# Four 64-row by 64-column products in place of two wide ones for the third hidden group, and one inverse transform moved ahead of a mix

## The chip, the cores and the metric

The kernel runs on one core of a Trainium2 chip. The metric is the device time in microseconds (us). TensorE (PE in the profile, PEld its weight loads), VectorE (DVE), ScalarE (ACT), GpSimd (POOL) and SyncE (SP) each work through a queue of their own and wait for one another by counting semaphores.

## The reference

A block of two residual parts over an image tensor (4, 48, 128, 128). `_ln_c` normalises over the 48 channels, `_ln_t` over the 48 channels of a token (a pixel).

```python
x = x + conv_part(_ln_c(x))        # conv_part, below
t = _to_tokens(x)                  # (4, 16384, 48)
t = t + ffn(_ln_t(t))
x = _from_tokens(t, x)

# conv_part(x): 3x3 convolution of the first 12 channels, 1x1 convolution 48 -> 254,
# 8x8 patches: rfft2, times fft_w, irfft2; halves a, b of 127 channels each;
# gelu(a) * b, 1x1 convolution 127 -> 48
# ffn(x): with q_mul = rounding to 5 exponent and 2 mantissa bits, q_acc to 5 and 10
h = relu(q_acc(q_acc(q_mul(x) @ q_mul(W1).T) + q_mul(b1)))    # 48 -> 192
y = q_acc(q_acc(q_mul(h) @ q_mul(W2).T) + q_mul(b2))          # 192 -> 48
```

## The kernel before

The images are cut into 32 bands of 16 rows (`STEPS`). A band's 16 rows are two bands of 8 rows laid on top of each other: partitions 0 to 47 hold the 48 channels of the upper, partitions 64 to 111 those of the lower (`HALF` is 64). Every step of the software pipeline works on seven bands at once, each in another stage: `live(t, d)` asks whether the band that is `d` behind exists, `at(t, d)` is its number. Steps 6 to 31 have all stages; before them the pipeline fills, after them it drains, and behind step 34 a separate `drain` works in half bands. The order of each engine's work within a step is written out by hand in that engine's `step` function, and waits on semaphore counts hold the engines together.

What stands around the change, for one step:

- `mix(t, s)`, s = 0 to 3: the 1x1 convolution to 254 channels for a quarter of the band, 16 matmuls of 60 rows (two row halves of the array at a time) into the PSUM pair `mixp` (or `misc0` and `misc1` for s = 1). `weigh(t, s)` on VectorE multiplies both banks by the frequency weights into `gmix[s % 2]`, and counts `gmix_ready` by two. Mix s waits for the weighing of s - 1 (mix 1, which has banks of its own, does not).
- `inverse(t, behind, s)`: the inverse transform of quarter s into `inva` (line 532, 8 matmul records) and `invb` (line 539, 8 records). `inva` waits for `gelu_ready` of quarter s - 1, `invb` for `h_ready` of quarter s - 1, which `gate` on VectorE counts. `gelu` on ScalarE turns `inva` into `gact`, and `gate` multiplies it with `invb` into `hbuf`.
- `turn_rest` transposes the first residual sum into `misc2` and `misc3` (line 663); `rest` on ScalarE copies it (`tpix`) and squares it (`tsq`); `second_norm` on VectorE (lines 1301 to 1313) makes the statistics from both, and GpSimd centres the tokens in between (line 1580, `tcen`), behind its addition into the output buffer (line 1538, `ob`).
- `hidden(t, c, g, dst)`: first layer of the feed-forward part for half c (512 pixels) of a band, output group g of three (line 619). The layer has 192 outputs for each of the two stacked bands, 384 in all. Groups 0 and 1 are outputs 0 to 127 of the upper and of the lower band, 48 rows each, in different row halves of the array. Group 2 is outputs 128 to 191 of both, by a block-diagonal weight of 112 rows and 128 columns. `accumulators` on ScalarE rounds the bank to `hid16`, `relu` on VectorE adds the bias, `activations` on ScalarE rounds to `hid8` in the next step, `second_layer` sums all three groups into `mixp`.
- `stream(t)`: the 3x3 convolution (line 568) into `misc3`; `convs` on ScalarE copies it, `convolve` (line 577) transposes it.

TensorE's order in the second half of a step, before: `turn_rest`, mix 2, hidden (0,0), hidden (0,1), `inva` of quarter 1, hidden (0,2) into `misc2`, `invb` of quarter 1, `stream`, mix 3, hidden (1,0), (1,1), (1,2), `convolve`, inverse of quarter 2; then the next step begins with the transposes of line 784.

ScalarE's order there: `tokens`, `rest`, accumulators (0,0) to (0,2), gelu of quarter 1, `convs`, accumulators (1,0) to (1,2), `zpix` (line 1122), gelu of quarter 2.

VectorE's order there: gate 0, weigh 2, `second_norm`, relu of half 0, gate 1, weigh 3, relu of half 1, gate 2.

Of the kernel before, what the change touches and what calls it, by code (L numbers as in the profile page):

```python
# [10 lines left out]
ALU = mybir.AluOpType  # L11
# [69 lines left out]
def metaformer_kernel(nc, x, w_pc, w_in, fft_w, w_out, w1, b1, w2, b2, fwd_d, inv_d, sel_d, eye_d, out):  # L81
    with ExitStack() as ctx:
# [404 lines left out]
        def _(pe):  # L487
# [111 lines left out]
            def rows(t, behind):  # L599
# [7 lines left out]
                if a < ROWS_EARLY:  # L607
                    pe.wait_ge(tsq_ready, upto(2 * m + 2))
                else:
                    pe.wait_ge(gmix_ready, upto(8 * n + 2))  # L610
                    pe.wait_ge(y16_ready, upto(2 * at(t, 6) + 2))
                dst = bank[3] if a < ROWS_EARLY else mixp[0]
                pe.transpose(dst[0:32, 0:128], rm[:].rearrange("p a j i -> p (a j i)"), eye[:])\
                  .then_inc(rmT_done, 1)

            def hidden(t, c, g, dst):

                r0, r1 = ((0, CH), (HALF, SPAN), (0, SPAN))[g]
                pe.matmul(dst[:], l1h[r0:r1, g, :], q16[r0:r1, 4 * c:4 * c + 4, :], start=True, stop=True,  # L619
                          skip_group_check=True).then_inc(hid_done, 1)  # L620

            def second_layer(t):
# [6 lines left out]
                for c in range(2):  # L629
                    for g in range(2):  # L630
                        r0 = HALF * g
                        pe.matmul(pair[c][r0:r0 + HALF, :], l2[:, g, r0:r0 + HALF], hid8[:, 3 * c + g, :],  # L632
                                  start=True, stop=False, skip_group_check=True)
                for c in range(2):
# [3 lines left out]
                    for r0 in (0, HALF):  # L638
                        mm = pe.matmul(pair[c][r0:r0 + HALF, :], l2[:, 2, r0:r0 + HALF], hid8[:, 3 * c + 2, :],  # L639
                                       start=False, stop=True, skip_group_check=True)  # L640
                    mm.then_inc(y_done, 1)
# [26 lines left out]
            def drain():  # L668
# [20 lines left out]
                def first_layer(k, c, dst):  # L689
                    pe.wait_ge(q16_ready, 2 * k + c + 1)  # L690
                    for g in range(3):
                        hidden(t, c, g, dst[g])

                def second_layer_half(c, dst):
                    for g in range(2):
# [9 lines left out]
                pe.wait_ge(lo_ready, 2 * STEPS)  # L705
                pe.wait_ge(h_ready, 4 * NEW + 2)
                project_half(0, bank[3])

                def between():
                    pe.wait_ge(hid8_ready, 6 * OLDER + 3)  # L710
                    second_layer_half(0, mixp[0])

# [9 lines left out]
                pe.wait_ge(y16_ready, 2 * OLDER + 1)  # L722
                second_layer_half(1, mixp[0])
                pe.wait_ge(tpix_ready, 2 * NEW + 1)
# [36 lines left out]
            def step(t):  # L761
# [14 lines left out]
                if live(t, 0):  # L776
# [5 lines left out]
                    pe.wait_ge(xord_ready, upto(a + 1))  # L782
                    for i in range(PAIRS):
                        mm = pe.transpose(bank[i // 4][:, (i % 4) * 128:(i % 4) * 128 + XSPAN],  # L784
                                          xord[:, i * PX:(i + 1) * PX], eye[0:XSPAN, 0:XSPAN])
# [72 lines left out]
                if a == 2:  # L858
# [25 lines left out]
        def _(act):  # L884
# [5 lines left out]

            def accumulators(t, c, groups):

                k = at(t, 5)
                for g in groups:
                    act.wait_ge(hid_done, upto(6 * k + 3 * c + g + 1))
                    act.wait_ge(hid8_ready, upto(6 * (k - 1) + 3 * c + g + 1))
                    act.activation(hid16[:, 3 * c + g, :], bank[g][:], ACT.Copy).then_inc(hid16_ready, 1)  # L897

            def activations(k, c, groups):

                for g in groups:
                    act.wait_ge(relu_ready, upto(6 * k + 3 * c + g + 1))
                    if c == 0 and g == 0:
                        act.wait_ge(y_done, upto(2 * k))
                    act.sem_inc(act_held, 1)
                    act.activation(hid8[:, 3 * c + g, :], hid16[:, 3 * c + g, :], ACT.Copy, saturate=False)\  # L906
                       .then_inc(hid8_ready, 1)
# [72 lines left out]
            def drain():  # L980

                def convert(k, c, g, tile=None):
                    act.wait_ge(relu_ready, 6 * k + 3 * c + g + 1)
                    act.wait_ge(y_done, 2 * (k - 1) + c + 1)
                    act.activation(hid8[:, 3 * c + g, :], hid16[:, 3 * c + g, :], ACT.Copy, saturate=False)\
# [72 lines left out]
            def step(t):  # L1058
# [29 lines left out]
                if live(t, 6):  # L1088
                    activations(l, 0, range(3))
                    activations(l, 1, range(3))  # L1090
                if live(t, 6):
# [42 lines left out]
        def _(dve):  # L1134
# [134 lines left out]

            def relu(t, c, parts=((0, 2), (2, 1))):  # L1270

                k = at(t, 5)
                for g, size in parts:
                    dve.wait_ge(hid16_ready, upto(6 * k + 3 * c + g + size))
                    buf = hid16[:, 3 * c + g:3 * c + g + size, :]
                    dve.tensor_scalar(buf, buf, bq[:, g // 2:g // 2 + 1], 0.0, ALU.add, ALU.max)\
                       .then_inc(relu_ready, size)

# [36 lines left out]
            def drain():  # L1315
# [57 lines left out]
                def convert(k, c, g):  # L1373
                    dve.wait_ge(relu_ready, 6 * k + 3 * c + g + 1)
                    dve.wait_ge(y_done, 2 * (k - 1) + c + 1)
                    dve.tensor_copy(hid8[:, 3 * c + g, :], hid16[:, 3 * c + g, :], saturate=False).then_inc(late_hid8, 1)
# [47 lines left out]
            def step(t):  # L1424
# [56 lines left out]
                if live(t, 3):  # L1481
                    gate(t, 3, 0)
                if live(t, 3):
                    weigh(t, 2)
                if live(t, 4):
                    second_norm(t)
# [163 lines left out]
```

## Time and profile before

| | |
|---|---|
| timed runs, median of 3 | 700.97 us (700.77 to 700.98) |
| profiled execution, first to last instruction (span) | 699.4 us |
| busy share of the span | PE 95%, PEld 76%, DVE 85%, ACT 77%, POOL 65% |
| granted TensorE clock, mean | 0.980 of full speed |

No separate time of the profiled execution stands in the profile; its span is 1.6 us under the median of the timed runs, and this much is taken as what lies around it. Engine busy shares are averages; a busy PE counts pipelined matmuls, so that the start-to-start distances of blocks of matmuls say more than their durations.

### The profile page before, as it was taken

The numbers are of one execution on the slowest core, as the hardware profiler recorded it, in microseconds if no ns is written. First come the engines' busy times: TensorE is split into PE (matmuls) and PEld (weight loads), VectorE is DVE, ScalarE is ACT, GpSimd is POOL, SyncE is SP. The second block draws the span as 40 slices with busy tenths as digits, with TensorE's granted clock in tenths as the row PEclk, the third lists the DMA queues.
The fourth block names the chain that finished last, engine by engine and source line by source line (L and its number), as shares of the span: only waits on it lengthen the run. The fifth ranks groups of instructions, "written<-read, shape, count | busy, mean of one in ns | idle before, by whom it ended". The sixth has DMA issues, their size and how long they took to land.

```text
span 699.4 us, 19176 instructions
## 1 busy us (share of the span) xinstructions
PE 666.5 (95%) x6620; PEld 529.3 (76%) x6620; DVE 597.9 (85%) x1159; ACT 536.8 (77%) x1087; POOL 456.9 (65%) x347
## 2 busy tenths in 40 slices
PE   4879999999999999999999999999999999999984
PEld 4657877778778877787878877787788777887751
DVE  7637889988988899988988899889888999877877
ACT  4244568888888888888889888888888888877784
POOL 2605677767777777677776877677777876753353
PEclk9989999999999999999999999999999999999995
DMA  4434445444544554445444544545445543342102
GB/s 102 79 78 118 121 113 131 112 126 128 142 120 118 142 140 121 114 120 138 127 123 131 139 131 107 132 121 144 121 116 144 139 129 103 100 119 87 47 23 68
DMA packets 52207, 80.73 MB, mean 115 GB/s; under 512 B 20823, under 2 KB 36079, under 8 KB 52111
## 3 DMA queue, kind: packets, MB, share of 16 engines
q1 hardware_dynamic: 50031, 78.56, 43.2%
q10 hardware_dynamic: 2080, 0.94, 0.6%
q8 instruction: 54, 0.88, 0.6%
q14 instruction: 42, 0.34, 0.2%
HBM read 63.17 MB, written 16.30 MB: 114 GB/s over the span
## 4 chain that ended last, share of the span: by engine, by line
PE 87%; DVE 3%; DMA 3%; issue 2%; ACT 1%; SPq 1%; POOL 1%; DVEq 0%; ACTq 0%; POOLq 0%
PE inva L532 17%; PE invb L539 15%; PE mixp L519 13%; PE misc L548 8%; PE misc L803 8%; PE misc L619 4%; PE misc L519 4%; PE misc L663 3%; PE misc L784 3%; PE misc L568 2%; PE misc L577 2%; PE misc L653 2%; PE mixp L632 2%; PE mixp L639 2%; DMA xin<-in_x_dram 1%
## 5 line engine op out<-in xcount | busy, mean ns | idle before, releaser
L1555 POOL TENSOR_TENSOR st<-st,neg_half 128x16 f32<-128x16 f32 x32 | 93.3, 2915 | 129.2 <-DVE st L1459 129.2
L532 PEld LDWEIGHTS inva<-inv,gmix 128*127 128x127 f32 x1024 | 123.4, 191 | 25.3 <-issue 16.6
L532 PE MATMUL inva<-inv,gmix 128*127 128x128 f32 x1024 | 141.0, 281 | 0.6 <-DVE gmix L1234 0.6
L1234 DVE TENSOR_TENSOR gmix<-mixp,freq_w 128x508 f32<-128x508 f32 x192 | 122.6, 680 | 16.9 <-PE mixp L519 16.9
L539 PE MATMUL invb<-inv,gmix 128*127 128x128 f32 x1024 | 134.7, 274 | 0.1
L539 PEld LDWEIGHTS invb<-inv,gmix 128*127 128x127 f32 x1024 | 126.2, 191 | 2.1 <-DVE hbuf L1245 0.5
L897 ACT ACTIVATE hid<-misc 128x512 f16<-128x512 f32 x180 | 94.1, 599 | 17.7 <-PE misc L619 17.7
L1245 DVE TENSOR_TENSOR hbuf<-gact,invb 127x512 f32<-127x512 f32 x128 | 87.4, 683 | 22.2 <-ACT gact L889 17.7
L1584 POOL TENSOR_TENSOR st<-st,neg_half 128x16 f32<-128x16 f32 x31 | 95.4, 3077 | 16.4 <-DVE st L1313 15.9
L906 ACT ACTIVATE hid<-hid 128x512 fp8e5<-128x512 f16 x174 | 93.2, 619 | 0.0
L889 ACT ACTIVATE gact<-inva 127x512 f32<-127x512 f32 x128 | 77.5, 605 | 19.9 <-PE inva L532 19.3
L519 PE MATMUL mixp<-win,zh 60*128 60x254 f16 x768 | 89.9, 272 | 0.7 <-DVE gmix L1234 0.6
L519 PE MATMUL mixp<-win,zl 60*128 60x254 f16 x768 | 89.0, 267 | 0.0
L1538 POOL TENSOR_TENSOR ob<-tch,y 112x1024 f32<-112x1024 f32 x29 | 62.1, 2140 | 34.1 <-DVE y L1294 34.1
L977 ACT ACTIVATE y<-mixp 112x512 f16<-112x512 f32 x58 | 31.4, 594 | 47.0 <-PE mixp L639 47.0
L803 PE MATMUL misc<-fwd,zpix 128*124 128x128 f32 x512 | 62.1, 275 | 0.0
L548 PE MATMUL misc<-hbuf,wout 127*64 127x512 f32 x248 | 60.1, 605 | 0.0
L803 PEld LDWEIGHTS misc<-fwd,zpix 128*124 128x124 f32 x512 | 58.6, 188 | 0.0
L519 PEld LDWEIGHTS mixp<-win,zh 60*128 60x128 f16 x768 | 37.1, 93 | 26.8 <-issue 14.5
L1435 DVE TENSOR_REDUCE st<-xpix 128x16 f32<-128x768 f32 x32 | 30.5, 952 | 28.3 <-ACT xpix L1068 28.3
L1580 POOL TENSOR_TENSOR tcen<-tpix,st 128x768 f32<-128x768 f32 x31 | 45.7, 1475 | 12.5 <-DVE st L1301 9.6
L1068 ACT ACTIVATE xpix<-misc 128x384 f32<-128x384 f32 x64 | 31.6, 494 | 23.2 <-PE misc L784 22.1
(184 smaller groups left out, 1358.2 us busy)
## 6 DMA issues: line engine op xcount, KB each, us to landing
taps<-cz_scratch SPq DMA_DIRECT2D x63, 292.2 KB
xin<-in_x_dram SPq DMA_DIRECT2D x64, 192.0 KB, 3.3
xres<-in_x_dram SPq DMA_DIRECT2D x64, 192.0 KB, 4.1
out_dram<-ob SPq DMA_DIRECT2D x60, 192.0 KB, 2.6
taps<-cz_scratch SPq DMA_DIRECT2D x63, 146.1 KB
crm<-rm_scratch SPq DMA_DIRECT2D x58, 96.0 KB
cx<-in_x_dram SPq DMA_DIRECT2D x32, 96.0 KB
cz_scratch<-cz SPq DMA_DIRECT2D x63, 48.8 KB
```

The lines of the kernel that those rows point to most:

```text
L519: mm = pe.matmul(pair[q][:, e * HID2:(e + 1) * HID2], zpart[r0:r0 + KC, 2 * s + e, :], win[r0:r0 + KC, wpart, :], start=(e == 0 and zpart ...
L532: mm = pe.matmul(inva[0:HID, q * PX:(q + 1) * PX], gmix[:, s % 2, q, 0:HID], inv[:], start=True, stop=True, skip_group_check=True)
L539: mm = pe.matmul(invb[0:HID, q * PX:(q + 1) * PX], gmix[:, s % 2, q, HID:HID2], inv[:], start=True, stop=True, skip_group_check=True)
L548: mm = pe.matmul(dst[HALF * j:HALF * j + HALF, :], wout[:], hbuf[:, half, j, :, :], start=True, stop=True, skip_group_check=True)
L803: mm = pe.matmul(bank[(3, 0)[i // 4]][0:KSPAN, (i % 4) * PX:(i % 4 + 1) * PX], zpix[:, ring(t, 3), i, 0:KSPAN], fwd[:], start=True, stop=True,
L889: act.activation(gact[:, s % 2], inva[0:HID, :], ACT.Gelu).then_inc(gelu_ready, 1)
L897: act.activation(hid16[:, 3 * c + g, :], bank[g][:], ACT.Copy).then_inc(hid16_ready, 1)
L906: act.activation(hid8[:, 3 * c + g, :], hid16[:, 3 * c + g, :], ACT.Copy, saturate=False)\
L1234: dve.tensor_tensor(gmix[:, s % 2, 2 * q:2 * q + 2, 0:HID2], pair[q][:, 0:2 * HID2].rearrange("p (e c) -> p e c", e=2), freq_w[:], ALU.mul ...
L1245: dve.tensor_tensor(hbuf[:, s // 2, :, 2 * e:2 * e + 2, :], gact[:, s % 2].rearrange("p (j i c) -> p j i c", j=2, i=2), invb[0:HID, :].rea ...
L1555: pool.tensor_tensor(st1[:, 6, :], st1[:, 5, :], neg_half[:], ALU.pow).then_inc(pow1, 1)
L1584: pool.tensor_tensor(st2[:, 6, :], st2[:, 5, :], neg_half[:], ALU.pow).then_inc(pow2, 1)
```

## The change

The third group of the first layer is now computed by `hidden_rest`, once for both halves of the band: four matmuls of 48 rows and 64 columns, each in one quadrant of the array, the lower band into `misc3` and the upper into `misc2`, half c of the band at output partitions 64 c. `hid16` and `hid8` keep six slots in a new order: slots 0 and 1 are half 0, slots 2 and 3 the third group of the lower and of the upper band, slots 4 and 5 half 1. The second layer follows (`rest_product`). `inverse(t, 3, 1)` stands ahead of mix 2 in one piece. `stream` now also waits for `hid16_ready`, 6 k + 3, since `misc3` is read by the third accumulator copy of the step. ScalarE has gelu 1 ahead of the accumulators, four of which now stand in one row ahead of `convs`. VectorE's order becomes gate 0, `second_norm`, gate 1, weigh 2, relu of slots 0 and 1, weigh 3, relu of slots 2 and 3, relu of slots 4 and 5, gate 2.

```diff
@@ stream(t)
+                if live(t, 5):
+                    pe.wait_ge(hid16_ready, 6 * at(t, 5) + 3)
                 pe.wait_ge(col_in, upto(64 * (c + 1)))
...
+            def hidden_rest(t):
+
+                for c in range(2):
+                    for j in (1, 0):
+                        r0 = HALF * j
+                        mm = pe.matmul(bank[2 + j][HALF * c:HALF * c + HALF, :], l1h[r0:r0 + CH, 2, r0:r0 + HALF],
+                                       q16[r0:r0 + CH, 4 * c:4 * c + 4, :], start=True, stop=True,
+                                       skip_group_check=True)
+                        if c == 1:
+                            mm.then_inc(hid_done, 1)
...
+            def rest_product(dst, c, j):
+
+                r0, o = HALF * c, HALF * j
+                return pe.matmul(dst[o:o + HALF, :], l2[:, 2, r0:r0 + HALF], hid8[:, (3, 2)[j], :],
+                                 start=False, stop=True, skip_group_check=True)
...
@@ TensorE, step(t)
                 if live(t, 3):
+                    inverse(t, 3, 1)
+                if live(t, 3):
                     pe.wait_ge(y16_ready, upto(2 * l + 2))
...
-                def last_group():
-                    if live(t, 0) and 3 <= a < ROWS_EARLY:
-                        rows(t, 0)
-                    if live(t, 5):
-                        pe.wait_ge(tsq_ready, upto(2 * m + 1, 2 * STEPS))
-                        hidden(t, 0, 2, bank[2])
-
-                if live(t, 3):
-                    inverse(t, 3, 1, last_group)
-                else:
-                    last_group()
+                if live(t, 5):
+                    pe.wait_ge(tsq_ready, upto(2 * m + 2, 2 * STEPS))
+                    hidden_rest(t)
+                if live(t, 0) and 3 <= a < ROWS_EARLY:
+                    rows(t, 0)
...
                     hidden(t, 1, 1, bank[1])
-                    pe.wait_ge(hid16_ready, upto(6 * k + 3))
-                    hidden(t, 1, 2, bank[2])
@@ ScalarE
-                    act.activation(hid16[:, 3 * c + g, :], bank[g][:], ACT.Copy).then_inc(hid16_ready, 1)
+                    act.activation(hid16[:, g, :], bank[(0, 1, 3, 2, 0, 1)[g]][:], ACT.Copy).then_inc(hid16_ready, 1)
...
+                if live(t, 3):
+                    gelu(t, 3, 1)
                 if live(t, 5):
-                    accumulators(t, 0, (0,))
+                    accumulators(t, (0, 1))
+                if live(t, 5):
+                    accumulators(t, (2, 3))
                 if live(t, 0) and 3 <= a < ROWS_EARLY:
                     rows(t, 0)
-                if live(t, 5):
-                    accumulators(t, 0, (1, 2))
-                if live(t, 3):
-                    gelu(t, 3, 1)
...
-                    accumulators(t, 1, range(3))
+                    accumulators(t, (4, 5))
@@ VectorE
                     gate(t, 3, 0)
-                if live(t, 3):
-                    weigh(t, 2)
                 if live(t, 4):
                     second_norm(t)
+                if live(t, 3):
+                    gate(t, 3, 1)
+                if live(t, 3):
+                    weigh(t, 2)
                 if live(t, 5):
                     relu(t, 0)
-                if live(t, 3):
-                    gate(t, 3, 1)
                 if live(t, 3):
                     weigh(t, 3)
                 if live(t, 5):
                     relu(t, 1)
+                    relu(t, 2)
```

The drain's waits and its older half of the second layer follow the new slots.

## Rows read from the trace of the kernel before

**Rows 1.** The page: the span, and each engine's busy time.
```profile
span 699.4 us, 19176 instructions
PE 666.5 (95%) x6620; PEld 529.3 (76%) x6620; DVE 597.9 (85%) x1159; ACT 536.8 (77%) x1087; POOL 456.9 (65%) x347
```

**Rows 2.** The chain that ended last, middle of one step: start, us, what.
```profile
351.77 1.08 PE inva L532 x8
352.85 0.22 PE misc L619
...
355.51 0.54 PE misc L619 x3
...
356.49 0.89 PE inva L532 x8
```

**Rows 3.** Timeline of the same step, TensorE: start, us, engine, line, what.
```profile
338.32 0.83 PE L784 MATMUL misc<-eye,xord 96*128 96x96 f32 x8
...
350.50 0.28 PE L519 MATMUL mixp<-win,zh 60*128 60x254 f16 x2
...
353.89 0.65 PE L568 MATMUL misc<-taps,wpc 108*32 108x512 f16 x8
354.47 0.28 PE L519 MATMUL mixp<-win,zh 60*128 60x254 f16 x2
...
355.35 0.70 PE L619 MATMUL misc<-q,l1h 48*128 48x512 f16 x3
...
358.10 0.82 PE L784 MATMUL misc<-eye,xord 96*128 96x96 f32 x8
```

**Rows 4.** Timeline of the same step, ScalarE.
```profile
352.19 0.48 ACT L967 ACTIVATE tsq<-misc 128x384 f32<-128x384 f32 x1
352.55 1.55 ACT L897 ACTIVATE hid<-misc 128x512 f16<-128x512 f32 x3
353.98 0.60 ACT L889 ACTIVATE gact<-inva 127x512 f32<-127x512 f32 x1
...
355.76 1.57 ACT L897 ACTIVATE hid<-misc 128x512 f16<-128x512 f32 x3 [0.58 <-PE misc L619]
```

**Rows 5.** Timeline of the same step, VectorE.
```profile
350.70 0.68 DVE L1245 TENSOR_TENSOR hbuf<-gact,invb 127x512 f32<-127x512 f32 x1
...
353.81 0.80 DVE L1307 SCALAR_TENSOR_TENSOR st<-st 128x16 f32<-128x16 f32 x1
354.65 0.17 DVE L1310 SCALAR_TENSOR_TENSOR st<-st 128x16 f32<-128x16 f32 x1
...
355.60 0.68 DVE L1245 TENSOR_TENSOR hbuf<-gact,invb 127x512 f32<-127x512 f32 x1
356.20 1.27 DVE L1234 TENSOR_TENSOR gmix<-mixp,freq_w 128x508 f32<-128x508 f32 x2
```

**Rows 6.** Timeline of the same step, GpSimd.
```profile
350.86 2.14 POOL L1538 TENSOR_TENSOR ob<-tch,y 112x1024 f32<-112x1024 f32 x1 [0.36 <-DVE y L1294]
353.11 1.48 POOL L1580 TENSOR_TENSOR tcen<-tpix,st 128x768 f32<-128x768 f32 x1
```

**Rows 7.** Timeline of step 32, the first without new input.
```profile
629.55 1.47 POOL L1580 TENSOR_TENSOR tcen<-tpix,st 128x768 f32<-128x768 f32 x1 [2.02 <-DVE st L1301]
```

**Rows 8.** Windows while the pipeline fills: stretch, us, busy (count) of PE, PEld, DVE, ACT, POOL, clock.
```profile
29.59:33.00 3.41, 3.41 (x19) 3.41 (x18) 2.65 (x8) 2.00 (x10) 3.22 (x4) 0.50 0.64 177
33.00:39.82 6.82, 2.99 (x27) 2.18 (x26) 0.32 (x1) 0.73 (x1) 1.34 (x1) 1.00 0.98 193
39.83:46.65 6.82, 5.96 (x22) 4.77 (x23) 1.13 (x4) 2.05 (x6) 0.00 (x0) 0.50 0.14 38
```

**Rows 9.** Timeline of TensorE around its second fall in clock.
```profile
37.17 0.65 PE L568 MATMUL misc<-taps,wpc 108*32 108x512 f16 x8 [2.48 <-DMA taps<-cz_scratch]
37.75 0.71 PE L583 MATMUL misc<-eye 128*128 128x128 f32 x4
40.69 1.11 PE L577 MATMUL misc<-eye,convs 128*128 128x128 f32 x4 [2.22 <-ACT convs L1114]
```

More of the change, by code:

```diff
@@ L611, in rows @@
                     pe.wait_ge(y16_ready, upto(2 * at(t, 6) + 2))
+                if live(t, 5) and a < ROWS_EARLY:
+                    pe.wait_ge(hid16_ready, 6 * at(t, 5) + 3)
                 dst = bank[3] if a < ROWS_EARLY else mixp[0]
@@ L629, in second_layer @@
                 for c in range(2):
[L630 to L634, printed above, removed]
                     if c == 1:
@@ L637, in second_layer @@
                         pe.sem_inc(pe_held, 1)
-                    for r0 in (0, HALF):
-                        mm = pe.matmul(pair[c][r0:r0 + HALF, :], l2[:, 2, r0:r0 + HALF], hid8[:, 3 * c + 2, :],
-                                       start=False, stop=True, skip_group_check=True)
+                    for g in range(2):
+                        r0 = HALF * g
+                        pe.matmul(pair[c][r0:r0 + HALF, :], l2[:, g, r0:r0 + HALF], hid8[:, 4 * c + g, :],
+                                  start=True, stop=False, skip_group_check=True)
+                for c in range(2):
+                    for j in range(2):
+                        mm = rest_product(pair[c], c, j)
                     mm.then_inc(y_done, 1)
@@ L692, in first_layer, with older_half @@
                         hidden(t, c, g, dst[g])
+                def older_half(c, dst):
+                    for g in range(2):
+                        r0 = HALF * g
+                        pe.matmul(dst[r0:r0 + HALF, :], l2[:, g, r0:r0 + HALF], hid8[:, 4 * c + g, :],
+                                  start=True, stop=False, skip_group_check=True)
+                    for j in range(2):
+                        mm = rest_product(dst, c, j)
+                    mm.then_inc(y_done, 1)
                 def second_layer_half(c, dst):
@@ L706, in drain @@
                 pe.wait_ge(h_ready, 4 * NEW + 2)
+                pe.wait_ge(hid16_ready, 6 * OLDER + 3)
                 project_half(0, bank[3])
                 def between():
-                    pe.wait_ge(hid8_ready, 6 * OLDER + 3)
-                    second_layer_half(0, mixp[0])
+                    pe.wait_ge(hid8_ready, 6 * OLDER + 4)
+                    older_half(0, mixp[0])
                 inverse(t, 4, 3, between)
@@ L722, in drain @@
                 pe.wait_ge(y16_ready, 2 * OLDER + 1)
-                second_layer_half(1, mixp[0])
+                older_half(1, mixp[0])
                 pe.wait_ge(tpix_ready, 2 * NEW + 1)
@@ L783, in step @@
                     for i in range(PAIRS):
+                        if i == 4 and not peeled:
+                            pe.wait_ge(hid16_ready, upto(6 * l + 6))
                         mm = pe.transpose(bank[i // 4][:, (i % 4) * 128:(i % 4) * 128 + XSPAN],
@@ L889, in gelu, with accumulators, activations @@
                 act.activation(gact[:, s % 2], inva[0:HID, :], ACT.Gelu).then_inc(gelu_ready, 1)
-            def accumulators(t, c, groups):
+            def accumulators(t, groups):
                 k = at(t, 5)
                 for g in groups:
-                    act.wait_ge(hid_done, upto(6 * k + 3 * c + g + 1))
-                    act.wait_ge(hid8_ready, upto(6 * (k - 1) + 3 * c + g + 1))
-                    act.activation(hid16[:, 3 * c + g, :], bank[g][:], ACT.Copy).then_inc(hid16_ready, 1)
-            def activations(k, c, groups):
+                    act.wait_ge(hid_done, upto(6 * k + g + 1))
+                    act.wait_ge(hid8_ready, upto(6 * (k - 1) + g + 1))
+                    act.activation(hid16[:, g, :], bank[(0, 1, 3, 2, 0, 1)[g]][:], ACT.Copy).then_inc(hid16_ready, 1)
+            def activations(k, groups):
                 for g in groups:
-                    act.wait_ge(relu_ready, upto(6 * k + 3 * c + g + 1))
-                    if c == 0 and g == 0:
+                    act.wait_ge(relu_ready, upto(6 * k + g + 1))
+                    if g == 0:
                         act.wait_ge(y_done, upto(2 * k))
                     act.sem_inc(act_held, 1)
-                    act.activation(hid8[:, 3 * c + g, :], hid16[:, 3 * c + g, :], ACT.Copy, saturate=False)\
+                    act.activation(hid8[:, g, :], hid16[:, g, :], ACT.Copy, saturate=False)\
                        .then_inc(hid8_ready, 1)
@@ L983, in convert @@
                     act.wait_ge(relu_ready, 6 * k + 3 * c + g + 1)
-                    act.wait_ge(y_done, 2 * (k - 1) + c + 1)
+                    act.wait_ge(y_done, 2 * (k - 1) + (c + 1 if k == NEW else 2))
                     act.activation(hid8[:, 3 * c + g, :], hid16[:, 3 * c + g, :], ACT.Copy, saturate=False)\
@@ L1088, in step @@
                 if live(t, 6):
-                    activations(l, 0, range(3))
-                    activations(l, 1, range(3))
+                    activations(l, range(6))
                 if live(t, 6):
@@ L1268, in rows, with relu @@
                 dve.tensor_tensor(rm[:, 1], order(6), order(2), ALU.mult).then_inc(mr_ready, 1)
-            def relu(t, c, parts=((0, 2), (2, 1))):
+            def relu(t, i):
                 k = at(t, 5)
[L1273 to L1277, printed above, removed]
+                dve.wait_ge(hid16_ready, upto(6 * k + 2 * i + 2))
+                buf = hid16[:, 2 * i:2 * i + 2, :]
+                dve.tensor_scalar(buf, buf, bq[:, i % 2:i % 2 + 1], 0.0, ALU.add, ALU.max).then_inc(relu_ready, 2)
             def scale_tokens(t):
@@ L1374, in convert @@
                     dve.wait_ge(relu_ready, 6 * k + 3 * c + g + 1)
-                    dve.wait_ge(y_done, 2 * (k - 1) + c + 1)
+                    dve.wait_ge(y_done, 2 * (k - 1) + (2 if k == OLD else c + 1))
                     dve.tensor_copy(hid8[:, 3 * c + g, :], hid16[:, 3 * c + g, :], saturate=False).then_inc(late_hid8, 1)
@@ L1482, in step @@
                     gate(t, 3, 0)
+                if live(t, 4):
+                    second_norm(t)
+                if live(t, 3):
+                    gate(t, 3, 1)
                 if live(t, 3):
                     weigh(t, 2)
-                if live(t, 4):
-                    second_norm(t)
                 if live(t, 5):
                     relu(t, 0)
-                if live(t, 3):
-                    gate(t, 3, 1)
                 if live(t, 3):
```

## The prediction

> **What bounds the kernel now.** I read the page first: TensorE is busy for 95% of the span and no other engine above 85% [rows 1]. The chain that ended last, read through one step, is almost all TensorE, block upon block [rows 2]; the reader is to see that a block there costs its start-to-start distance. One step runs from the transposes at 338.32 to those at 358.10, so a full step takes 19.78 us [rows 3]. TensorE has next to no pause in it. So a saving on TensorE counts in full, and so does every new pause, because nothing later in the step stands idle to absorb it. The other engines' timelines of the same step say how far they run ahead of TensorE, and that decides the change, since it reorders them.
>
> I give all times below as places in this one step. The first part of the step, up to the end of `turn_rest` at 350.50 (where mix 2 starts now, [rows 3]), is untouched but for the order of second-layer products.
>
> **TensorE's own work.** Before, group 2 costs one product of 0.22 for half 0 [rows 2] and one of the three products that take 0.54 together after mix 3 [rows 2]. Two products of different row halves take one pass of 0.22, so the third costs 0.22 with a gap of 0.10 beside. Together 0.44 leaves. The quadrant products are not in the trace. Their floor is one pass, 0.22, if all four run together; their ceiling is four passes, 0.88. I take 0.22, plus 0.10 for a gap like the one just seen; both ends turn out to be hidden. The trace does not show what a change between row halves, quadrants and column strips costs beyond such gaps. The Trainium skill, TensorEngine Tiling (Array Packing), section Key Properties, states that a change of tiling mode drains the engine. This speaks against the change, which adds a mode between two others; by it the sum would rise by a gap or two per step, and these would lie in the pause below, so it stays as it is.
>
> **The moved inverse.** `inva` of quarter 1 can start at 350.50: its weighing and gelu 0 are long done. It takes 0.89, or 1.08 after products of another shape (its two rows in [rows 2]), to 351.4. `invb` wants gate 0, which ends at 350.70 + 0.68 = 351.38 [rows 5]: no real wait, 0.1 at most. So `invb` is through at 352.4, mix 2 at 353.3 (a mix takes 354.47 to 355.35, 0.88, [rows 3]), hidden (0,0) and (0,1) at 353.5, the quadrants at 353.85, or 354.5 if they run one by one. Before, stream starts at 353.89 [rows 3]; TensorE would be there at the same time with less work left behind it.
>
> **The new wait of stream.** Stream writes `misc3`, and now waits for the third accumulator copy. ScalarE ends `tsq` at 352.67 [rows 4], does gelu 1 (0.60, [rows 4]) to 353.2, and then waits for hidden (0,0). Its first copy comes 0.41 after the start of these products (355.35 to 355.76, [rows 3, 4]): 353.3 + 0.41 = 353.7. Three copies take 1.55 [rows 4]: 355.27. So stream starts at 355.27 instead of 353.89, 1.38 late, and TensorE stands idle for some 1.3 to 1.4. Queued behind it are mix 3, the half-1 products, `convolve` and the inverse of quarter 2. This pause covers the quadrant products even at four passes: at 354.5 plus their latency the third copy, due to start at 354.75, still has its input. Without this cover the ceiling would cost 0.66 a step. Stream itself takes 0.58 (353.89 to 354.47, [rows 3]), to 355.85.
>
> **The next thing late: weigh 2.** Mix 3 needs `gmix_ready` of weigh 2. Before, weigh 2 stood ahead of `second_norm`. Now VectorE does gate 0 to 351.38, then `second_norm`, gate 1, and only then weigh 2. `second_norm` contains line 1307, an instruction over 16 elements that takes 0.80, while its like on line 1310 takes 0.17 [rows 5]. It ends at 354.61, and GpSimd's `tcen` ends at 353.11 + 1.48 = 354.59 [rows 6]: the small instruction waits for GpSimd. `tcen` stands behind `ob`, which ends at 353.00, so it can't come more than 0.1 earlier, although VectorE reaches `second_norm` sooner. I take `second_norm` to end where it does today. Then gate 1 starts when the relu does now, at 354.95, and takes the 0.60 start to start that it takes ahead of weigh 3, and the two weighings 1.27 (355.60, 356.20, [rows 5]): weigh 2 ends at 354.95 + 0.60 + 1.27 = 356.8. Mix 3 starts there instead of at 354.47 [rows 3]: 2.33 late, of which 1.38 is stream's wait and 0.95 this one. The Trainium skill, SBUF — State Buffer, section SBUF: two separate sides, says that VectorE instructions with two SBUF inputs and GpSimd lock a shared port pair for a whole instruction, and the other is blocked. By that rule line 1307 is blocked again to the end of `tcen`; the trace agrees (0.80 beside 0.17).
>
> **The rest of the step.** After mix 3 the product block loses one pass: 0.54 becomes 0.32, minus 0.22. `convolve` finds `convs` ready (355.85 + 0.2 + 0.6). ScalarE's last two copies end near 359.15, `zpix` near 359.6, gelu 2 near 360.2, and the next transposes start at 358.10 + 2.11 = 360.2: they fit as they do now. Weigh 3 starts as long after mix 3 as today. The three relus of 1024 columns in place of two and two halves cost VectorE 0.3 in a place where it waits. So a full step becomes 19.78 + 2.33 - 0.22 = 21.9 us.
>
> **The sum.** 26 full steps by 2.11: +54.9. Steps 32 and 33: `tcen` waits for VectorE there, 2.02 idle before it [rows 7], so it moves forward with `second_norm` and mix 3 is set by stream alone: 1.3 - 0.2, about 1.1 each, +2.2. Step 34 has no stream but waits for weigh 2: +1.7. Steps 3 to 5 have the new VectorE order, and step 5 the new copies too: 0.5, 0.9 and 1.7 by the same walk, +3.1, uncertain by 2. The drain changes by tenths. Together +61.9: a span of 761.3, and with the 1.6 us around it 762.9.
>
> **The clock.** Each step then has two pauses of TensorE, 1.3 to 1.4 before stream and 0.95 before mix 3, with 0.58 of work between. While the pipeline fills, the clock is at its lower level (1.2 GHz) from 29.59 to 33.00 and from 39.83 to 46.65, at 2.4 GHz between [rows 8]. Before the second fall the engine had worked for about 1.3 us (37.17 to 38.46) after a pause of 2.48, and stood again for 2.22 [rows 9]. It fell after or in the second pause and not after the first. So of two pauses of this size one lowered it. Mine are as long only together, with work between; I choose one full step in three, 8 of 26, and this is the weakest number here. The shortest low stretch lasted 3.41 with TensorE busy throughout [rows 8]; as mix 3 and all behind it are TensorE-bound, half of it is lost, 1.7. So 8 by 1.7 is +13.6: 776.5.
>
> **The rivals, their times and chances.**
> - *The forecast, pauses and some falls:* 776 (768 to 795), 38%.
> - *Pauses, and the clock stays up:* 763 (757 to 768), 36%. For it: the single pauses are shorter than any before a fall. Against: their sum. The Trainium skill, TensorE: Matmul & The Clock Gate, section Why this matters for your kernels, ties a fall to one long pause between bursts; by it this rival holds. The trace disagrees in part, as it fell around a pause of 2.22.
> - *Line 1307 isn't blocked:* it takes 0.17, and `second_norm` starts up to 0.25 sooner. Weigh 2 ends near 355.9, just behind stream: 355.95 - 354.47 - 0.22 = 1.25 a step, 26 by 1.25 plus 6: 739, with less reason for the clock to fall; 13%. Against it stands the 0.80.
> - *The clock falls in every step:* 26 by 1.7 is 44 on 763: 807; 10%.
> - *Not slower:* the one mechanism is that ScalarE's third copy and weigh 2 are done when TensorE comes for them. It decides if the copy ends by 353.9, 1.4 earlier than my walk, and weigh 2 by 354.5, 2.3 earlier. Then 0.44 leaves and 0.32 comes, 26 by 0.12: 698. The copy can't start before hidden (0,0), so I give it 3%.
> - *The quadrants run one after another,* so that the change does not do what it says: it lies under the pause and changes none of these times. It is a part of each case.
>
> The likeliest gives 776. The range takes in the two pause cases, most of the upper part of the third, and leaves out the last two, about 2 in 10: 742 to 795. What this kernel's timing can tell from no change is about 0.2%, 1.4 us. Faster 3%, same 1%, slower 96%.
>
> **What would show it.** In the chain or the waits: TensorE idle before line 568, released by ScalarE's accumulator copies, about 1.3 a step, and idle before mix 3, released by weigh 2, about 0.9. In the timeline: line 1307 still at 0.80, and a period of 21.9. The granted clock: 1.00 throughout (763) or low stretches of some 3.4. Wrong would be: no wait before line 568, a `tcen` that starts well before 353, or a step whose other half now has a wait of its own that I left out.

## The result

| | before | changed |
|---|---|---|
| median of the timed runs | 700.94 us (5 runs) | 805.81 us (804.73 to 808.1, 5 runs) |
| ratio | | 1.151 (95% interval 1.150 to 1.153) |
| span of the profiled execution | 699.4 us | 803.7 us |
| mean granted TensorE clock | 0.980 | 0.932 |

The changed kernel is 105 us slower, and its time lies outside the forecast's range (742 to 795). The page of the changed kernel, its span, busy times and the clock by slices:

```profile
span 803.7 us, 19299 instructions
PE 705.6 (88%) x6680; PEld 554.6 (69%) x6680; DVE 618.1 (77%) x1129; ACT 545.4 (68%) x1087; POOL 453.7 (56%) x347
...
PEclk9889999999999899999989999998999999999995
```

TensorE's share has fallen from 95% [rows 1] to 88%, and the clock row has an 8 here and there in the middle. The waits of the changed kernel between 124 and 690 us (who waited for whom: us in total, times, longest):

```profile
PEld misc L570 <- issue: 43.3, 24, 1.9
PE misc L570 <- ACT hid L923: 36.9, 24, 1.6
...
PEld mixp L519 <- DVE gmix L1259: 27.8, 25, 1.1
PE mixp L519 <- DVE gmix L1259: 14.7, 25, 0.6
```

Both waits of the forecast are there, once a step: line 570 (stream; 568 before) for ScalarE's copy, 1.5 each, and mix 3 for weigh 2 (line 1259; 1234 before). The weight loads' rows (PEld) count the same pauses again. One step of the changed kernel at full clock, TensorE's timeline, to be held against [rows 3]:

```profile
375.95 1.06 PE L532 MATMUL inva<-inv,gmix 128*127 128x128 f32 x8
376.97 1.15 PE L539 MATMUL invb<-inv,gmix 128*127 128x128 f32 x8
...
378.94 0.38 PE L634 MATMUL misc<-q,l1h 48*128 48x512 f16 x2
379.25 0.41 PE L625 MATMUL misc<-q,l1h 48*64 48x512 f16 x4
381.18 0.65 PE L570 MATMUL misc<-taps,wpc 108*32 108x512 f16 x8 [1.53 <-ACT hid L923]
382.43 0.28 PE L519 MATMUL mixp<-win,zh 60*128 60x254 f16 x2 [0.60 <-DVE gmix L1259]
...
383.31 0.38 PE L634 MATMUL misc<-q,l1h 48*128 48x512 f16 x2
```

The four quadrant products (line 625) start within 0.01 of one another and take 0.41 together, where one of them takes 0.40. Then TensorE does nothing until 381.18. In the same step on VectorE (compare [rows 5]) and GpSimd ([rows 6]):

```profile
377.94 0.61 DVE L1324 SCALAR_TENSOR_TENSOR st<-tpix,st 128x16 f32<-128x16 f32 x1 [1.03 <-ACT tpix L990]
...
379.34 0.80 DVE L1330 SCALAR_TENSOR_TENSOR st<-st 128x16 f32<-128x16 f32 x1
380.18 0.17 DVE L1333 SCALAR_TENSOR_TENSOR st<-st 128x16 f32<-128x16 f32 x1
...
380.50 0.69 DVE L1270 TENSOR_TENSOR hbuf<-gact,invb 127x512 f32<-127x512 f32 x1
381.10 1.27 DVE L1259 TENSOR_TENSOR gmix<-mixp,freq_w 128x508 f32<-128x508 f32 x2
```

```profile
376.40 2.13 POOL L1562 TENSOR_TENSOR ob<-tch,y 112x1024 f32<-112x1024 f32 x1 [0.36 <-DVE y L1317]
378.64 1.48 POOL L1604 TENSOR_TENSOR tcen<-tpix,st 128x768 f32<-128x768 f32 x1
```

Line 1330 again takes 0.80 and ends at 380.14, with `tcen` at 380.12, as line 1324 does with `ob` just before (378.55 and 378.53); weigh 2 ends at 382.37, and mix 3 starts at 382.43. The windows of three consecutive steps of the changed kernel and of one low stretch (us, busy (count) of PE, PEld, DVE, ACT and POOL, granted clock):

```profile
340.90:364.53 23.63, 21.50 (x208) 17.09 (x206) 18.47 (x34) 17.02 (x35) 14.38 (x11) 0.93 0.41 108
364.53:386.55 22.02, 19.89 (x207) 15.78 (x206) 18.75 (x34) 16.95 (x35) 13.74 (x10) 1.00 0.43 113
386.55:411.58 25.03, 22.91 (x208) 18.16 (x206) 18.68 (x34) 17.02 (x35) 15.05 (x12) 0.86 0.42 104
403.99:410.81 6.82, 6.35 (x38) 5.32 (x39) 3.29 (x6) 2.66 (x5) 4.15 (x5) 0.50 0.63 147
```

A step takes 22.02 at 2.4 GHz, 23.63 with one low stretch of 3.41 at 1.2 GHz, 25.03 with one of 6.82. By these lengths 16 of the 26 full steps have a short low stretch, 3 a double one and 7 none.

**Where the 104.3 us between the spans went**, by the distances between the starts of the coefficient matmuls (line 803, 835 in the changed kernel), step by step:

| term | forecast | measured |
|---|---|---|
| 26 full steps, at full clock | 26 by 2.11 = 54.9 | 26 by 2.25 = 58.5 |
| steps 3 to 5 | 3.1 | 4.9 |
| steps 32 and 33 | 2.2 | 2.9 |
| step 34 and the drain | 1.7 | 3.5 |
| the clock in the full steps | 13.6 | 34.5 |
| together | 75.5 | 104.3 |

The measured clock term is the lengthening of the 26 full steps, 93.0, less 58.5. The row of the drain holds some clock too: from 772.6 to 776.0 the changed kernel's clock is 0.50, which by the price of such a stretch is 1.6 of the 3.5.

### The profile page after: what moved, and what is told of

It reads as the page before. It is cut to its first block, busy times and chain, and to the rows that moved or that the text cites. A ratio compares the mean times of both kernels' runs of the same rounds, so it can differ in the third digit from the quotient of the medians.

```text
span 803.7 us, 19299 instructions
## 1 busy us (share of the span) xinstructions
PE 705.6 (88%) x6680; PEld 554.6 (69%) x6680; DVE 618.1 (77%) x1129; ACT 545.4 (68%) x1087; POOL 453.7 (56%) x347
## 4 chain that ended last, share of the span: by engine, by line
PE 65%; DVE 15%; issue 8%; ACT 6%; DMA 2%; POOL 1%; SPq 1%; ACTq 0%; DVEq 0%; POOLq 0%
PE inva L532 13%; PE invb L539 11%; PE mixp L519 9%; PE misc L548 7%; PE misc L835 7%; DVE gmix L1259 4%; PE misc L579 3%; ACT tpix L990 3%; PE misc L519 3%; DVE st L1328 3%; PE misc L816 2%; DVE st L1330 2%; DVE st L1324 2%; PE mixp L656 2%; PE misc L673 2%
## 5 line engine op out<-in xcount | busy, mean ns | idle before, releaser
L1579 POOL TENSOR_TENSOR st<-st,neg_half 128x16 f32<-128x16 f32 x32 | 93.3, 2916 | 217.5 <-DVE st L1482 217.5
L532 PE MATMUL inva<-inv,gmix 128*127 128x128 f32 x1024 | 151.8, 296 | 1.1 <-DVE gmix L1259 1.1
L532 PEld LDWEIGHTS inva<-inv,gmix 128*127 128x127 f32 x1024 | 138.0, 210 | 16.3 <-DVE gmix L1259 12.3
L539 PE MATMUL invb<-inv,gmix 128*127 128x128 f32 x1024 | 140.9, 282 | 1.5 <-DVE hbuf L1270 1.5
L539 PEld LDWEIGHTS invb<-inv,gmix 128*127 128x127 f32 x1024 | 128.2, 197 | 5.9 <-DVE hbuf L1270 1.9
L519 PE MATMUL mixp<-win,zh 60*128 60x254 f16 x768 | 96.9, 285 | 17.8 <-DVE gmix L1259 17.7
L1608 POOL TENSOR_TENSOR st<-st,neg_half 128x16 f32<-128x16 f32 x31 | 90.2, 2910 | 16.4 <-DVE st L1336 16.4
L519 PE MATMUL mixp<-win,zl 60*128 60x254 f16 x768 | 97.4, 284 | 0.0
L570 PE MATMUL misc<-taps,wpc 108*32 108x512 f16 x256 | 21.2, 406 | 49.1 <-ACT hid L923 43.1
```

The costliest lines, as they stand in the source:

```text
L519: mm = pe.matmul(pair[q][:, e * HID2:(e + 1) * HID2], zpart[r0:r0 + KC, 2 * s + e, :], win[r0:r0 + KC, wpart, :], start=(e == 0 and zpart ...
L532: mm = pe.matmul(inva[0:HID, q * PX:(q + 1) * PX], gmix[:, s % 2, q, 0:HID], inv[:], start=True, stop=True, skip_group_check=True)
L539: mm = pe.matmul(invb[0:HID, q * PX:(q + 1) * PX], gmix[:, s % 2, q, HID:HID2], inv[:], start=True, stop=True, skip_group_check=True)
L1579: pool.tensor_tensor(st1[:, 6, :], st1[:, 5, :], neg_half[:], ALU.pow).then_inc(pow1, 1)
L1608: pool.tensor_tensor(st2[:, 6, :], st2[:, 5, :], neg_half[:], ALU.pow).then_inc(pow2, 1)
```

## The experiments

Two theories stood against each other after the result. One: the two new waits make pauses, and these lower the clock in nearly every step, which is what the forecast had too small. The other: the time is all waits, and the moved inverse or the quadrant products cost something of their own. Each ratio is taken against the kernel before on the same chip, whose median is 700.81, 700.92 and 700.55 us for the three sets of runs.

**Idle matmuls in both pauses.**

```diff
+            def fill(t, count):
+                pe.wait_ge(gelu_ready, upto(4 * at(t, 3) + 2))
+                keep_busy(count, inva)
...
                     hidden_rest(t)
+                    fill(t, 6)
...
+                    fill(t, 3)
                 if live(t, 3):
                     mix(t, 3)
```

> The changed kernel with idle matmuls (128x128 f32 on the identity, into inva once gelu 1 has read it) in TensorE's two pauses: six ahead of the wait of stream, three ahead of mix 3. They add no output. Theory (what the forecast lacks is the clock: the two pauses lower it in nearly every step): the granted clock stays at 1.00 through the full steps, the steps keep their pauses' length, about 22.1 us each, and the time is 764 to 772. Rival 1 (the lost time is waits, and a low clock only goes with them): 795 to 806, low stretches as before. Rival 2 (the fillers themselves delay stream): above 806.

Measured: 778.9, ratio 1.109 (1.097 to 1.120). TensorE's timeline of one step, and a window over 22 steps, which for the changed kernel has a clock of 0.94 (an idle product leaves two records, so that x12 and x6 are the six and the three):

```profile
347.17 0.41 PE L630 MATMUL misc<-q,l1h 48*64 48x512 f16 x4
347.51 1.60 PE L585 MATMUL inva<-eye 128*128 128x128 f32 x12
349.11 0.65 PE L570 MATMUL misc<-taps,wpc 108*32 108x512 f16 x8
349.69 0.94 PE L585 MATMUL inva<-eye 128*128 128x128 f32 x6
```

```profile
150.00:640.00 490.00, 489.92 (x4921) 395.55 (x4921) 409.39 (x728) 373.23 (x749) 318.31 (x243) 1.00 0.44 114
```

The clock is up through all full steps. A step takes 22.23, as the second filler runs some 0.2 over; the first steps, which had a low stretch of 6.8 here, begin the full ones 3.6 later than in the changed kernel. Together that is why the time is 7 above the range. It is still 27 us less than that of the changed kernel: more useless work, less time. The rival of waits alone is out.

**Weigh 2 first again.**

```diff
                 if live(t, 3):
                     gate(t, 3, 0)
+                if live(t, 3):
+                    weigh(t, 2)
                 if live(t, 4):
                     second_norm(t)
                 if live(t, 3):
                     gate(t, 3, 1)
-                if live(t, 3):
-                    weigh(t, 2)
```

> The changed kernel with weigh 2 on VectorE ahead of second_norm again, as in the kernel before. Theory: mix 3 no longer waits for weigh 2 but only for stream, so a full step at full clock loses 0.67 of its 22.03 and takes about 21.4; the remaining pause is too short for the clock to fall in most steps: 745 to 752. If the clock still falls as often: about 783. Rival (weigh 2 wasn't what mix 3 waited for): 800 to 806.

Measured: 769.64, ratio 1.095 (1.083 to 1.107). At full clock a step takes 21.36, 0.67 less: the wait of mix 3 is the size that was read. But up to 550 us every other step takes 22.96 or 23.06, with a low stretch of 3.4. Stream's pause alone (1.5) still lowers the clock, in 11 of the 26 full steps, which I had not expected, and the time lies between the two that were named. Two steps running:

```profile
324.30:345.60 21.30, 21.30 (x205) 16.94 (x201) 16.07 (x31) 15.37 (x32) 13.69 (x11) 0.92 0.41 102
345.60:367.00 21.40, 19.78 (x209) 15.73 (x205) 17.68 (x34) 16.90 (x35) 14.33 (x11) 1.00 0.46 117
```

**The same with the first pause filled.** The edit is that of `x2_weigh` with the six idle matmuls ahead of stream, and none ahead of mix 3.

> x2_weigh with the six idle matmuls in the pause ahead of stream. x2_weigh still showed 13 low stretches, one in two steps. Theory (each low stretch costs 1.6 and has no other effect): none in the full steps, 21.4 to 21.5 a step, 748 to 756. Rival: 765 or more.

Measured: 750.7, ratio 1.071 (1.068 to 1.074). 21.36 a step, clock 1.00 between 150 and 640. Of the 18.9 us between the two runs, the 26 full steps hold 17.4. In 11 of them (ten of 22.96 or 23.06, and step 31) `x2_weigh` lost 1.6 each, which is 17.6. So a short low stretch costs 1.6 (1.7 in the forecast), and nothing else of size hangs on it.

**Both waits shortened.** The edit of `x2_weigh`, and:

```diff
-                    accumulators(t, (0, 1))
-                if live(t, 5):
-                    accumulators(t, (2, 3))
+                    accumulators(t, (2, 0, 1, 3))
...
-                    pe.wait_ge(hid16_ready, 6 * at(t, 5) + 3)
+                    pe.wait_ge(hid16_ready, 6 * at(t, 5) + 1)
```

> The changed kernel with weigh 2 ahead of second_norm (as x2_weigh, 21.36 a step at full clock) and with misc3 copied first, so that stream waits for one copy behind the quadrant products and not for three behind hidden (0,0). Theory (both waits named in the forecast, and nothing else, make the pauses): stream starts 0.9 sooner, a full step takes 20.4 to 20.6, the clock stays up, 723 to 730. Rival (the moved inverse brings another bound that then shows): 21.0 a step or more, 735 to 745.

Measured: 735.59, ratio 1.049 (1.047 to 1.052); 20.73 a step, clock up in all full steps. 0.63 less than with weigh 2 alone, where 0.9 was expected: the waits between 150 and 650 show what is left of stream's,

```profile
PE misc L570 <- ACT hid L923: 21.9, 24, 1.0
```

0.91 a step. The two waits are the mechanism, as stream's 0.91 is nearly all of the 0.95 by which this step is still longer than the kernel before's. The gain was overestimated, and slow first steps (8.4 behind those of the kernel before, 3.5 behind those of the changed kernel) add to the time. The time lies in the rival's range (735 to 745), the step does not (20.73, where the rival wanted 21.0 or more).

**The quadrants alone**, in the place of hidden (0,2), all else in the order of before:

```diff
-                if live(t, 3):
-                    inverse(t, 3, 1)
...
+                def last_group():
+                    if live(t, 5):
+                        pe.wait_ge(tsq_ready, upto(2 * m + 2, 2 * STEPS))
+                        hidden_rest(t)
...
+                if live(t, 3):
+                    inverse(t, 3, 1, last_group)
```

> The quadrant products alone, where hidden (0,2) stood between the two halves of inverse 1, with the inverse, ScalarE's gelu 1 and VectorE's order as in the kernel before; stream's wait on the third copy is kept, and the fourth copy stands behind gelu 1. Theory (four quadrants take one pass; the price of the change is in the moved inverse and its orders): one pass of 0.22 is saved per step and stream waits about 0.2: 697 to 703, no clock falls. Rival (quadrants one after another, or a drain for each change of tiling): 708 to 720.

Measured: 709.65 (10 runs), ratio 1.013 (1.011 to 1.014), 20.08 a step: 0.30 more than before, where none was expected; the time lies in the rival's range. There is no gain. The chain of the step shows why, beside [rows 2]:

```profile
355.94 1.08 PE inva L532 x8
357.02 0.34 PE misc L625 x4
357.36 1.08 PE invb L539 x8
358.44 0.09 issue
358.53 0.65 PE misc L570 x8
```

The pass of four takes 0.34 where the wide product takes 0.22, and `invb` behind it 1.08 where a block of eight takes 0.89. The 1.08 is what [rows 2] show for a block that follows products of another shape. Together that is 0.31 more, against about 0.2 that the missing wide product saves behind mix 3. The rest is stream, which finds `misc3` read about 0.2 late.

**The inverse alone.** The kernel before with `inverse(t, 3, 1)` in one piece ahead of mix 2 and gelu 1 ahead of the copies; the third group as it was.

> The kernel before with the inverse of quarter 1 in one piece ahead of mix 2 and gelu 1 ahead of the accumulator copies, nothing else: third group as two wide products into misc2, VectorE's order of before, and so no new wait of stream. Theory: mix 3 waits some 0.4 for weigh 2, as mix 2 and weigh 2 now lie right before it, and invb of quarter 2 waits some 0.7 for gate 1, which is behind second_norm and relu: about 20.9 a step, 725 to 732, clock up. Rival (the moved inverse costs nothing, all of the loss is the new copies' wait): 699 to 703.

Measured: 743.2, ratio 1.058 (1.047 to 1.069), 21.01 a step (20.9 expected), clock up in the full steps. Both waits that were named are there, `invb` of quarter 2 for gate 1 and mix 3 for weigh 2, between 150 and 640 us:

```profile
PE invb L539 <- DVE hbuf L1244: 9.9, 23, 0.4
PE mixp L519 <- DVE gmix L1233: 7.4, 23, 0.3
```

The idle time alone is 0.75 of the 1.23. The first steps add 5.8, which puts the time above the range. So the moved inverse costs 1.2 a step with no quadrant product in the kernel and VectorE's order as before.

**The third copy first**, in `x3_quads`: `accumulators(t, (2, 0, 1))`, and stream waits for one copy.

> The quadrant products alone (as x3_quads, 20.08 a step), with ScalarE copying misc3, the bank that stream writes, first of the three copies, so that stream finds it free. Theory: x3_quads lost 0.26 a step to this wait and the rest of its loss to the quadrants themselves (0.34 for the pass where a wide product had 0.22, and a later start): 19.8 to 19.9 a step, 701 to 704. Rival (the wait is only shown there and the loss is the changes of tiling): 708 to 711, as x3_quads.

Measured: 716.88, ratio 1.022 (1.021 to 1.024), 20.28 a step: outside theory and rival both. Its ScalarE row:

```profile
362.52 1.57 ACT L927 ACTIVATE hid<-misc 128x512 f16<-128x512 f32 x3 [0.57 <-PE misc L625]
```

ScalarE, which before went straight from `tsq` to hidden (0,0) [rows 4], now waits 0.57 for the later product, and all behind it is late: `convolve` waits 0.28 for `convs`. A copy that is asked for first is no help if it is ready last.

**Wide products in the quadrants' place**, in `x3_quads`. The second layer takes the third group of the other half of the band here and in `x12_wideorder`; the work is the same.

```diff
-                for c in range(2):
-                    for j in (1, 0):
...
+                for c in (1, 0):
+                    pe.matmul(bank[2 + c][:], l1h[0:SPAN, 2, :], q16[0:SPAN, 4 * c:4 * c + 4, :],
+                              start=True, stop=True, skip_group_check=True).then_inc(hid_done, 1)
```

> x3_quads with the four quadrant products replaced by the two wide products of the kernel before (112 rows, 128 columns), both in the same place, half 1 into misc3 and half 0 into misc2; all else equal. Theory (four quadrants run at once in one pass, and entering and leaving the split of the array costs some 0.1 each time, so that four in quadrants cost what two wide ones cost): 20.0 to 20.1 a step, 707 to 712, no difference from x3_quads. Rival 1 (one pass really is saved): 20.3, 714 or more. Rival 2 (the quadrants are what x3_quads lost by): 19.8, 701 to 703.

Measured: 708.71, ratio 1.011 (1.010 to 1.013), 20.08 a step, the same as with quadrants. Two wide products take 0.47 in its chain and `invb` behind them 0.89; four quadrants 0.34 and 1.08. But this pair can't tell the two forms apart by its time: in both, stream starts 0.26 after ScalarE's third copy (ends at 358.28 and 357.33, starts at 358.53 and 357.59), so that ScalarE sets the step and hides a difference of TensorE. The next pair has no such wait.

**Mix 3 ahead of stream**, in `x3_quads`, with `convolve` between the halves of inverse 2; and the same with wide products.

> x3_quads with mix 3 ahead of stream, and convolve between the two halves of inverse 2, gelu 2 ahead of the copy to zpix. Stream then comes 0.9 later and finds misc3 read. Theory (x3_quads loses 0.26 a step to stream's wait and nothing to the quadrants themselves): 19.7 to 19.8 a step, 698 to 703. Rival (ScalarE, whose work is now later against TensorE, becomes the next wait): 20.1 or more, 708 and up.

> x10_order with the two wide products in place of the quadrants (as x9_wide). Theory (quadrants and wide products cost the same here): the time of x10_order within 2, at 698 to 703. Rival 1 (quadrants save a pass where nothing waits behind them): 5 more than x10_order. Rival 2 (they cost more): 3 or more below it.

Measured: 711.49, ratio 1.015 (1.014 to 1.017), and 709.65, ratio 1.013 (1.011 to 1.014); 20.07 and 20.01 a step in the first half and 0.17 more in the second, where expectations were 19.7 to 19.8. Both times are in the range of the rival of `x10_order` (708 and up), but ScalarE is not the reason: no wait of TensorE for it is left. They lie within 2 of each other, as the theory of `x12_wideorder` had it. Stream's wait is gone, as forecast, yet the step is no shorter. The chain of `x10_order`, and the two blocks of `x12_wideorder` that differ:

```profile
356.15 0.34 PE misc L625 x4
356.49 1.08 PE invb L539 x8
357.57 0.98 PE mixp L519 x16
358.55 0.58 PE misc L570 x8
359.13 0.32 PE misc L634 x2
359.45 1.08 PE inva L532 x8
```

```profile
355.85 0.47 PE misc L623 x2
356.33 0.89 PE invb L539 x8
```

Hidden (1,0) and (1,1) cost 0.32 behind the column strips of stream where they cost 0.22 behind a mix, and `inva` 1.08 where it cost 0.89 behind `convolve`. Each new neighbour of another shape takes 0.1 to 0.2. The quadrants with `invb` behind them take 1.42, the two wide products with theirs 1.36, and the 0.06 between them is the 0.06 between the steps, 1.6 of the 1.8 us between the medians (whose runs don't overlap: 711.2 to 711.8 and 709.2 to 709.9). So the pass that is saved is more than paid for at the two borders of the split.

**GpSimd's order**, twice, in the changed kernel: `output(t)` behind `tcen`, and behind the power as well.

> The changed kernel with GpSimd's tcen ahead of its addition into the output buffer, so that tcen ends as VectorE's reduction does and line 1307 (1330 in the changed kernel) is not held up. Theory (the small instruction waits for GpSimd's instruction to end): it takes about 0.2 in place of 0.80, weigh 2 and mix 3 come some 0.65 sooner, a full step at full clock takes about 21.4, and the time is 765 to 788 by how often the clock falls. Rival (0.80 is its own time, or another cause holds it): 22.0 a step, 803 to 808.

> The changed kernel with GpSimd's addition into the output buffer behind both tcen and the power of second_norm. x7_pool had it between them, and then the next small VectorE instruction, line 1333, took 2.05 beside it. Theory (a small VectorE instruction with two SBUF inputs ends with the GpSimd instruction that runs): 1333 takes 0.17 again, 1330 some 0.6, weigh 2 comes about 0.4 sooner than in the changed kernel: 21.6 a step at full clock, 770 to 795 by how often the clock falls. Rival (the addition holds up another VectorE instruction where it now stands, a relu or the bias): 22 a step or more, 800 or more.

Measured: 874.59, ratio 1.248 (1.245 to 1.251), and 804.53, ratio 1.148 (1.144 to 1.153). The first was a miss in the time and the best proof of the mechanism. VectorE and GpSimd in `x7_pool`:

```profile
404.53 0.59 DVE L1330 SCALAR_TENSOR_TENSOR st<-st 128x16 f32<-128x16 f32 x1
405.16 2.05 DVE L1333 SCALAR_TENSOR_TENSOR st<-st 128x16 f32<-128x16 f32 x1
```

```profile
403.62 1.47 POOL L1602 TENSOR_TENSOR tcen<-tpix,st 128x768 f32<-128x768 f32 x1 [2.16 <-DVE st L1324]
405.05 2.12 POOL L1562 TENSOR_TENSOR ob<-tch,y 112x1024 f32<-112x1024 f32 x1
```

1330 now ends with `tcen`, and the next small instruction ends with `ob`, at 407.2, so that gate 1, weigh 2 and mix 3 come later still. The step grew to 25.05 and 26.1, all with low stretches. In `x11_pool2` line 1333 is back at 0.18 and 1330 at 0.60, and its shortest steps take 21.60, 0.43 less than in the changed kernel, as forecast. But its time is the rival's (800 or more). Its 26 full steps are 40.1 us longer than 26 of 21.60. Low stretches stand in 16 of them, by their price 25.6. At least 5 of the rest are a wait that neither side named, here in TensorE's timeline:

```profile
353.35 0.84 PE L570 MATMUL misc<-taps,wpc 108*32 108x512 f16 x8 [3.47 <-DMA taps<-cz_scratch]
```

In four steps stream waits 2.0 to 3.5 for the DMA of its input, where its usual pause is 1.5. The addition now ends late, SyncE's queue stores its result ahead of the load of `crm` (lines 468 and 415), and GpSimd makes from `crm` the `cz` from which that input comes.

## Why the prediction was wrong

The direction and the two waits were right, the time was not: the forecast was 776, the measured time 806.

- *The moved inverse and the quadrants' place:* `invb`, mix 2 and hidden (0,0) came 0.1 to 0.2 after the walk's places, the quadrants 0.3. Right to that size.
- *The wait of stream:* stream was to start 4.77 after the end of `turn_rest`, and started 5.23 after it (381.18 less 375.95). The cause was the third copy, as named. 0.2 of the difference came with the late products, the rest, 0.3, lies between the end of the copy and the start of TensorE behind a wait, a term that the walk left out.
- *Weigh 2:* mix 3 was to come 6.3 after that point and came 6.48 after it. Line 1330 takes 0.80 again, as forecast, and `x7_pool` and `x11_pool2` show that GpSimd holds it. The lock that the prediction cited from the Trainium skill (SBUF — State Buffer, SBUF: two separate sides) agrees with both: each time the small instruction ends within 0.05 of GpSimd's. `x2_weigh` shows the step's share of this wait, 0.67 at full clock, as the later stream left less than 0.95 for it.
- *The rest of the step and the sum:* 22.03 against 21.9. `x1_fill` holds this step at 22.23 with its fillers' 0.2. Ends of the pipeline: 11.3 against 7.0.
- *The clock:* this is the step that failed. I took "one full step in three, 8 of 26", 13.6 us. It was 19 of 26, three of them doubly, and 34.5 us; the price of a fall was right (1.6). I had counted two pauses with work between as milder than one of their length, with nothing in the trace to say so, and took too few. `x2_weigh` shows that stream's pause alone is enough in 11 steps of 26. With 34.5 the forecast would have stood at 797, and the other sizes' small errors, 8, make the 806. The rival of a fall in every step (807) had 10%. That its number came out is in part luck: it counted 44 for the clock in 26 steps, where 19 had 34.5, and the 8 of the other terms filled the difference.
- *That the clock would not fall at all* had 36%, as no single pause was as long as one before a fall, and by the rule of one long pause that the prediction cited from the Trainium skill (TensorE: Matmul & The Clock Gate, Why this matters for your kernels). The trace disagrees with the rule here: the clock fell with pauses of 1.5 and 0.6, and in `x2_weigh` with 1.5 alone.
- *The quadrants cost 0.32 with their gap:* they take one pass, but `x10_order` and `x12_wideorder` show that with both borders they cost 0.06 more than two wide ones. The drain at a change of tiling mode that the Trainium skill states (TensorEngine Tiling (Array Packing), Key Properties), and which I set at nothing, as it lay under the pause, agrees with these borders; that they are a drain is not shown, only their price where no pause covers it. In the changed kernel it was covered, so the sum did not feel it.

What stays open: why a low stretch comes in one step and not in the next when the pauses are the same. And the full steps begin anywhere between 101.2 us (`x10_order`) and 110.1 (`x1_fill`), with low stretches at different places before them; this was not taken apart. No version tried beats the kernel before.

## What to carry to other kernels

Where TensorE sets the time, first ask of a reordering whether the engines behind it are as far ahead as before; here one matmul pass was to be won, and two waits of 1.5 and 0.6 were brought in. Price a repeated pause twice, once for itself and once for the clock: a third of this loss was the clock's, and idle matmuls in the pauses gave 27 us back without touching a wait. Count a split of the array by its borders too, since one pass saved between two whole-array blocks came out at nothing. And before work is moved later in one queue, look at what the other queues keep behind its result: moving one GpSimd addition cost waits at a small VectorE instruction in one place and at a DMA in the other.

## What the runs showed of the hardware

- Two pauses of TensorE, 1.5 and 0.6 long with 0.6 of work between, brought the clock to 1.2 GHz in 19 of 26 steps; the first alone did so in 11 of 26 (`x2_weigh`), and one of 0.9 to 1.0 in none (`x6_both`).
- A VectorE instruction over 16 elements took 0.18, 0.60, 0.80 or 2.05, by which GpSimd instruction ran beside it (0.18 and 0.60 in `x11_pool2`, 0.80 in the changed kernel, 2.05 in `x7_pool`).
- Four products in the four quadrants ran as one of 0.41; with the borders of the split they took 0.06 more than two wide ones (`x10_order` and `x12_wideorder`).
